# Rotating the queries of an attention and feed-forward kernel in blocks of four heads, moved through DRAM

## Chip, cores, metric

One core of a Trainium2 chip. The metric is the device time of one execution in microseconds (us); the lower the better.

## What is computed

Per batch (B = 4) of 256 tokens with 256 features: a cross-attention with 16 heads whose keys and values come from a latent of 64, with a rotated part of 64 beside the plain part of each head, then a feed-forward layer with ternary weights and quantised activations. Cut to what the change touches:

```python
kv_c = kv @ W_kvc                      # latent of 64
q_c = q @ W_dq                         # latent of 96
q_nope = (q_c @ W_uq).reshape(b, lq, H, HD).transpose(0, 2, 1, 3)   # H 16, HD 128
q_rope = (q_c @ W_qr).reshape(b, lq, H, R).transpose(0, 2, 1, 3)    # R 64
k_rope = kv_c @ W_kr
q_rope = _rope(q_rope, lq)             # [x1*cos - x2*sin, x1*sin + x2*cos], x1, x2 the halves of 32
k_rope = _rope(k_rope, lk)
scores = (einsum('bhqd,bkhd->bhqk', q_nope, k_nope) + einsum('bhqr,bkr->bhqk', q_rope, k_rope)) * scale
scores = where(good, scores, NEG)      # a window of 8 segment numbers
out = einsum('bhqk,bkhd->bqhd', softmax(scores), v).reshape(b, lq, H * HD) @ W_o
x = x + tanh(g_xattn) * out
x = x + tanh(g_ffn) * ffn(layernorm(x))  # 256 -> 1024 -> 256, silu, gelu, layer norm, quantised twice
```

## The kernel before

Tokens are worked on in F = 8 tiles of 128, and each tile in STEPS = 4 steps of GROUP = 4 heads, so there are N = 32 steps. Step n belongs to tile f = n // 4 and has k = n % 4. All segment numbers in use lie in the first 128 keys, so the branch with 128 keys runs (kts = 1). Head pairs share one operand: for an even head the partitions 0 to 63 of qcat and kcat hold the plain part (folded into the latent's 64) and 64 to 127 the rotated one; for an odd head it is the other way round.

Each engine has its own program, in an order written out by hand, and they meet at semaphores. One step n of the loop:

- TensorE: scores(n) (L878 adds the mask, L883 the four products with qcat), transpose_probs(n-2) (L895), project of a later step (L805 into bank_pair, four matmuls with wcat; L808 into bank_swap, two with wswap, whose columns are those of wcat with the halves exchanged), values(n-2) (L907). Between them lie the parts of the feed-forward of earlier tiles: transpose_x (L930) and up (L939) in step 0, attn_out (L920) in steps 1 and 2, transpose_h (L949) in steps 2 and 3, down (L959) in step 3.
- VectorE: softmax_max(n) (L1289), invert_sums(n-1) (L1297), turn_step: L1137 multiplies bank_pair by the cosines (ones for the plain parts) into qcat, L1141 multiplies bank_swap by the signed sines into turned. Then layer_norm_h (L1230, L1231) in step 0, the quantising of the hidden row (L1182, L1190, L1192, L1193) with silu (L1212) in step 1, the residual and its quantising in step 2, moments and output (L1260, L1264) in step 3. first_product (L1206) comes ahead of step 1.
- ScalarE: copy_latT (L633), copy_probT (L642), exponentials (L654, four with their sums). In step 1 the squares of the hidden row (L621) come before and the tanh (L606) behind the exponentials, in step 2 copy_h (L626) and gelu (L611) behind them; gelu needs another table, and so do the next exponentials. In tile 0 the absolute values of both feed-forward weights (L587) follow the exponentials of steps 0 and 1.
- GpSimd: normalise(n-1) (L485), add_rope_step: L406 and L408 add turned to the two rotated halves of qcat, one after the other. Roots (L430, L437) and factors (L456) for the quantisations.
- SyncE: all loads but four, in one queue, then the store of each output tile (L377).

The projection runs AHEAD = 2 steps ahead of the scores that use it: project in step n is that of step n + 2, and turn_step and add_rope_step likewise. scores(n) waits for pair_done, the end of L408. The next project waits for pair_turned, the end of L1141.

Before the loop: inputs are normed and transposed, keys and values projected and the keys rotated (turn_keys, L1075 to L1079; their latents copied by ScalarE in two copies of 64x256, L536 and L537), and the head weights are transposed, copied by ScalarE (L573, L574) and folded (L794), with project(0, 0) between fold(1) and fold(2) and project(0, 1) behind them. ScalarE's copies to L573 follow directly on the squares of the distances (L550).

## Time and profile before

| | |
|---|---|
| Three runs, median | 251.71 us (251.49 to 251.83) |
| The profiled execution: its time | 251.6 us |
| Its span | 249.8 us, 4518 instructions |
| TensorE busy | 210.2 us, 84% |
| TensorE weight loads (beside it) | 167.5 us, 67% |
| VectorE busy | 187.7 us, 75% |
| ScalarE busy | 155.6 us, 62% |
| GpSimd busy | 149.7 us, 60% |
| DMA | 12.40 MB, nearly all in the first 42 us |
| Granted TensorE clock, mean | 0.937; full up to the last fifth |

The span is what the engines' records cover; the execution's own time has 1.8 us more around it. The busy time of an engine is the sum of its instructions' durations, and neighbours on one engine can overlap at their ends, so where one instruction's cost is wanted, the distance between two starts says more. A released wait stands behind a row in brackets: the idle time of the engine just before that instruction, and the instruction that ended it. A matmul of fp32 has two records. The chain that ended last runs through TensorE for 45% of the span, VectorE 19%, GpSimd 12%, ScalarE 9%.

### The profile page before, as it was taken

To read this page: it belongs to the slowest core of one execution; us is meant where nothing else is said; L and a number is where in the kernel's file an instruction comes from. 1 tells how busy PE (TensorE), PEld (TensorE's weight loads), DVE (VectorE), ACT (ScalarE), POOL (GpSimd) and SP (SyncE) were. 2 spreads that over 40 slices of the span, in tenths; PEclk is the share of its full clock that TensorE was granted. 3 is DMA by queue.
4 is the path that set the end of the run, shared out by engine and by line. 5 is a ranking of instruction groups with operands and counts; after the bars stand their busy time and mean duration, and the time that the engine had idled before them with its cause. 6 is when DMAs were issued, how large, how long until landed. Compare 5 with 4: busy or idle time off the path is not lost.

```text
span 249.8 us, 4518 instructions
## 1 busy us (share of the span) xinstructions
PE 210.2 (84%) x1452; PEld 167.5 (67%) x1452; DVE 187.7 (75%) x430; ACT 155.6 (62%) x455; POOL 149.7 (60%) x222
## 2 busy tenths in 40 slices
PE   1799899999999999998998999899899746834453
PEld 1677788688978877886786888678678632513231
DVE  2587556689786679988988998898899842779761
ACT  2256627737557597759559875965887593849021
POOL 0415726639776469788787878778787832062630
PEclk9999999999999999999999999999999996775557
DMA  6999994000000000000000000000000000000001
GB/s 194 286 213 184 318 385 189 0 0 3 1 3 0 3 3 0 3 0 0 24 1 0 25 0 0 4 21 0 4 22 0 3 0 21 0 0 0 24 22 31
DMA packets 11357, 12.40 MB, mean 50 GB/s; under 512 B 3936, under 2 KB 10336, under 8 KB 11104
## 3 DMA queue, kind: packets, MB, share of 16 engines
q1 hardware_dynamic: 10432, 11.44, 16.6%
q10 hardware_dynamic: 896, 0.61, 0.8%
q8 instruction: 14, 0.23, 0.4%
q14 instruction: 15, 0.12, 0.2%
HBM read 11.00 MB, written 1.05 MB: 48 GB/s over the span
## 4 chain that ended last, share of the span: by engine, by line
PE 45%; DVE 19%; POOL 12%; issue 11%; ACT 9%; DMA 1%; DVEq 0%; SPq 0%; POOLq 0%
PE bank_pair L805 7%; PE bank_score L883 5%; PE bank_ff L920 4%; POOL h_small L430 4%; PE bank_lat L907 4%; PE bank_swap L808 3%; DVE z L1206 3%; PE bank_prob L895 3%; DVE h L1230 3%; POOL prob_room L485 3%; DVE neg_max L1289 3%; ACT prob_room L654 3%; PE bank_ff L959 3%; PE bank_ff L939 2%; POOL qcat L408 2%
## 5 line engine op out<-in xcount | busy, mean ns | idle before, releaser
L654 ACT ACTIVATE prob_room<-bank_score,neg_max 128x128 f32<-128x128 f32 x128 | 45.3, 369 | 23.5 <-DVE neg_max L1289 23.5
L485 POOL TENSOR_TENSOR prob_room<-prob_room,rsum 128x512 f32<-128x512 f32 x32 | 33.3, 1041 | 26.0 <-DVE rsum L1297 25.8
L406 POOL TENSOR_TENSOR qcat<-qcat,turned 64x256 f32<-64x256 f32 x32 | 30.8, 963 | 11.9 <-DVE turned L1141 11.8
L883 PEld LDWEIGHTS bank_score<-kcat,qcat 128*128 128x128 f32 x256 | 33.7, 192 | 2.3
L805 PE MATMUL bank_pair<-qcT,wcat 96*128 96x128 f32 x256 | 34.0, 276 | 0.0
L883 PE MATMUL bank_score<-kcat,qcat 128*128 128x128 f32 x256 | 33.7, 275 | 0.0
L642 ACT COPY probT_room<-bank_prob 128x512 f32<-128x512 f32 x32 | 19.0, 594 | 22.4 <-PE bank_prob L895 22.4
L920 PE MATMUL bank_ff<-m_sb,latT 128*128 128x256 f32 x128 | 31.9, 395 | 0.0
L805 PEld LDWEIGHTS bank_pair<-qcT,wcat 96*128 96x128 f32 x256 | 31.1, 192 | 0.4 <-DVE wcat L1126 0.2
L408 POOL TENSOR_TENSOR qcat<-qcat,turned 64x256 f32<-64x256 f32 x32 | 29.6, 924 | 2.5
L1137 DVE TENSOR_TENSOR qcat<-bank_pair,cst 128x512 f32<-128x512 f32 x32 | 21.6, 674 | 10.5 <-PE bank_swap L808 10.5
L907 PE MATMUL bank_lat<-probT_room,kvc 128*64 128x256 f32 x128 | 21.3, 413 | 9.2 <-ACT probT_room L642 9.2
L920 PEld LDWEIGHTS bank_ff<-m_sb,latT 128*128 128x128 f32 x128 | 23.9, 196 | 6.2 <-issue 3.4
L654 ACT ACTIVATION_READ_ACCUMULATOR prob_room<-bank_score,neg_max 128x1 f32 x128 | 26.4, 206 | 0.0
L1289 DVE TENSOR_REDUCE neg_max<-bank_score 128x4 f32<-128x512 f32 x32 | 21.8, 682 | 3.5 <-PE bank_score L883 3.3
L895 PE MATMUL bank_prob<-cst,prob_room 128*128 128x128 f32 x128 | 19.8, 278 | 1.8 <-POOL prob_room L485 1.8
L949 PE MATMUL bank_ff<-cst,h 128*128 128x128 f32 x64 | 12.2, 335 | 9.9 <-DVE h L1193 9.8
L808 PE MATMUL bank_swap<-qcT,wswap 96*128 96x128 f32 x128 | 19.5, 275 | 0.0
L949 PEld LDWEIGHTS bank_ff<-cst,h 128*128 128x128 f32 x64 | 9.2, 172 | 13.6 <-DVE h L1193 13.6
L895 PEld LDWEIGHTS bank_prob<-cst,prob_room 128*128 128x128 f32 x128 | 15.2, 144 | 2.5 <-POOL prob_room L485 2.4
L808 PEld LDWEIGHTS bank_swap<-qcT,wswap 96*128 96x128 f32 x128 | 16.9, 192 | 0.0
L907 PEld LDWEIGHTS bank_lat<-probT_room,kvc 128*64 128x64 f32 x128 | 6.4, 137 | 15.5 <-ACT probT_room L642 10.6
(163 smaller groups left out, 436.6 us busy)
## 6 DMA issues: line engine op xcount, KB each, us to landing
wo<-in_L_xattn_W_o SPq DMA_DIRECT2D x1, 2048.0 KB, 19.5
w_sb<-in_L_ffn_w SPq DMA_DIRECT2D x2, 1024.0 KB, 9.9
out_x<-y SPq DMA_DIRECT2D x8, 128.0 KB, 1.7
wuq<-in_L_xattn_W_uq SPq DMA_DIRECT2D x1, 768.0 KB, 11.5
ctx_all<-in_ctx ACTq DMA_DIRECT2D x2, 256.0 KB, 5.0
x_all<-in_x SPq DMA_DIRECT2D x2, 256.0 KB, 4.7
cst<-in_consts SPq DMA_DIRECT2D x1, 512.0 KB, 7.0
x_all<-in_x SPq DMA_DIRECT2D x1, 512.0 KB, 8.2
```

The costliest lines, as they stand in the source:

```text
L406: nc.gpsimd.tensor_tensor(odd, odd, add_odd, ALU.add).then_inc(pair_half, 1)
L408: nc.gpsimd.tensor_tensor(even, even, add_even, ALU.add).then_inc(pair_done, 1)
L485: nc.gpsimd.tensor_tensor(p, p, rsum[:, k % 2, :].unsqueeze(2).broadcast_to([P, GROUP, kts * P]), ALU.mult).then_inc(prob_scaled, 1)
L654: last = nc.scalar.activation(prob_of(n, kts)[:, j, :], src[:, j, :], ACT.Exp, bias=neg_max[:, k % 2, j:j + 1], accum_out=esum[:, k % 2, j ...
L805: nc.tensor.matmul(bank_pair[:, (2 * j + e) * P:(2 * j + e + 1) * P], wcat[:, 2 * k + j, e, :], src, start=True, stop=True)
L808: last = nc.tensor.matmul(bank_swap[:, j * P:(j + 1) * P], wswap[:, 2 * k + j, :], src, start=True, stop=True)
L883: last = nc.tensor.matmul(bank[:, j * kts * P:(j + 1) * kts * P], qcat[:, k, hh // 2, hh % 2, :], kcat[:, b, hh % 2, 0:kts * P], start=Fal ...
L895: last = nc.tensor.transpose(bank_prob[:, j * P:(j + 1) * P], prob_of(n, kts)[:, j, kt * P:(kt + 1) * P], eye)
L907: last = nc.tensor.matmul(bank_lat[o * KVC:(o + 1) * KVC, 0:2 * P].rearrange("p (j s) -> p j s", j=2), kvc1[:, b * KT + kt, :], probT[:, k ...
L920: last = nc.tensor.matmul(bank_ff[:, 0, 0:D], latT[:, j, :], m_sb[:, j, :], start=(j == 0), stop=(j == PAIRS - 1))
L1137: nc.vector.tensor_tensor(qcat[:, k, :, :, :], bank_pair[:, :].rearrange("p (j e s) -> p j e s", j=2, e=2), cos, ALU.mult)
L1289: nc.vector.tensor_reduce(neg_max[:, k % 2, :], score_banks(k, kts), AX.X, ALU.max, negate=True).then_inc(max_done, 1)
```

## The change

The queries' rotated parts are projected apart from the plain ones. For a step, two matmuls with wrope give the first halves of the rotated parts of four heads in one block of 128 partitions and the second halves in another, both in bank_swap; two matmuls with wnope give the plain parts in bank_pair. VectorE multiplies the two blocks by a table of cosines and sines in one operation (product), GpSimd adds once (rotated). The rotated parts now lie on other partitions than qcat wants, so SyncE stores the block to a DRAM tensor (rope_stage), waits for it, and loads it back in two transfers of 64 partitions to qcat (move_rope). The plain parts are copied from bank_pair to qcat by ScalarE, in two copies of 64 partitions (copy_nope), behind the exponentials of a step. AHEAD is 3 instead of 2. The rotated parts of the keys are kept in the order that the new transfers give. The tables grow from 1152 to 1920 columns. W_qr is loaded once, in whole rows, instead of twice in pieces of 64 columns. The two gates are loaded earlier, and the loads of w1, w2, b1, ln_g, ln_b and b2 are issued from ScalarE's queue, between its squares of the distances and its fold copies. The stores of the output wait in SyncE's program behind a later move.

Cut to its core: declarations, the keys' side and the preparation of wrope (which reorders W_qr's columns by halves of a head) are left out. product holds [partition, slot, first or second half of the result, first or second half of the input, token], rotated the two sums.

```diff
--- before.py
+++ after.py
     freq = (np.float32(1.0) / np.float32(10000.0) ** (np.arange(half, dtype=np.float32) / np.float32(half)))
     ang = np.arange(S, dtype=np.float32)[None, :] * freq.astype(np.float32)[:, None]
     cos, sin = np.cos(ang).astype(np.float32), np.sin(ang).astype(np.float32)
-    one = np.ones((KVC, S), np.float32)
+    cos4, sin4 = np.concatenate([cos] * 4), np.concatenate([sin] * 4)
     c = np.zeros((P, CONSTS), np.float32)
     c[:, EYE:EYE + P] = np.eye(P, dtype=np.float32)
     c[:, IOTA:IOTA + S] = np.arange(S, dtype=np.float32)[None, :] + LOOKBACK / 2
-    c[:, COS:COS + S] = np.concatenate([one, cos, cos])
-    c[:, COS + S:COS + 2 * S] = np.concatenate([cos, cos, one])
-    c[:, SIN:SIN + S] = np.concatenate([-sin, sin, -sin, sin])
+    for i, part in enumerate((cos4, -sin4, sin4, cos4)):
+        c[:, ROT + i * S:ROT + (i + 1) * S] = part
+    c[:, COS:COS + S] = np.concatenate([np.stack([cos, cos], 1).reshape(R, S)] * 2)
+    c[:, SIN:SIN + S] = np.concatenate([np.stack([-sin, sin], 1).reshape(R, S)] * 2)
     return c
 
 
...
             load(cst[:, IOTA:CONSTS], consts[:, IOTA:CONSTS], "rope")
             with nc.allow_non_contiguous_dma(reason="1024 token numbers"):
                 load(seg_i[:, :], itok.rearrange("b (t p) -> p (b t)", p=P), "seg")
+            load(gates[:, 0:1], g_xattn.partition_broadcast(P), "gate0")
+            load(gates[:, 1:2], g_ffn.partition_broadcast(P), "gate1")
             load_group(load, x_all, x_v, 2, "x")
             load_group(load, ctx_all, ctx_kv.rearrange("b (t p) d -> p (b t) d", p=P), 2, "ctx")
-            wqr_pair = W_qr.rearrange("k (j e n) -> k j e n", e=2, n=R)
-            load(wcat[:, :, 0, KVC:P], wqr_pair[:, :, 0, :], "wqr0")
-            load(wcat[:, :, 1, 0:R], wqr_pair[:, :, 1, :], "wqr1")
+            load(wqr[:, :], W_qr, "wqr")
             load(wuq[:, :, :], W_uq.rearrange("k (h n) -> k h n", h=H), "wuq")
             load(wuk, W_uk.rearrange("k (h n) -> k h n", h=H), "wuk")
             load(wuk_wuv[KVC:P, :, :], W_uv.rearrange("k (h n) -> k h n", h=H), "wuv")
             load(wo[:, :, :], W_o.rearrange("(h p) n -> p h n", p=P), "wo")
-            load(gates[:, 0:1], g_xattn.partition_broadcast(P), "gate0")
-            load(gates[:, 1:2], g_ffn.partition_broadcast(P), "gate1")
-            load(w1_sb[:, :, :], w1.rearrange("(c p) n -> p c n", p=P), "w1")
-            load(w2_sb[:, :, :], w2.rearrange("(c p) n -> p c n", p=P), "w2")
-            load(b1_bc[:, :], b1.partition_broadcast(P), "b1")
-            load(g_bc[:, :], ln_g.partition_broadcast(P), "g")
-            load(lb_bc[:, :], ln_b.partition_broadcast(P), "lb")
-            load(b2_bc[:, :], b2.partition_broadcast(P), "b2")
 
             out_v = out.rearrange("b (t p) d -> (b t) p d", p=P)
-            for f in range(F):
-                sp.wait_ge(y_done, f + 1)
-                sp.dma_start(out_v[f, :, :], y[:, :]).then_inc(out_stored, 16)
+            staged = stage.rearrange("k (j e i) o s -> k e (i o) j s", j=2, e=2)
+
+            def move_rope(n):
+
+                k = n % STEPS
+                sp.wait_ge(rope_rotated, n + 1)
+                if n >= STEPS:
+                    sp.wait_ge(score_ready, n - STEPS + 1)
+                sp.dma_start(stage[k, :, :, :], rotated[:, k, :, :]).then_inc(rope_staged, 16)
+                sp.wait_ge(rope_staged, 16 * (n + 1))
+                for e in range(2):
+                    lo = KVC if e == 0 else 0
+                    sp.dma_start(qcat[lo:lo + R, k, :, e, :], staged[k, e, :, :, :]).then_inc(rope_moved[k], 16)
+
+            def store(c):
+                sp.wait_ge(y_done, c + 1)
+                sp.dma_start(out_v[c, :, :], y[:, :]).then_inc(out_stored, 16)
+
+            for n in range(N):
+                move_rope(n)
+                c = (n - 4 * STEPS - AHEAD) // STEPS
+                if c >= 0 and n == c * STEPS + 4 * STEPS + AHEAD:
+                    store(c)
+            for c in range((N - 1 - 4 * STEPS - AHEAD) // STEPS + 1, F):
+                store(c)
             sp.wait_ge(out_stored, 16 * F)
 
         @block.gpsimd
         def _(pool):
-            rope = R // 2
             pool.wait_ge(consts_made, 1)
 
             def input_root(b):
...
                 add_rope(kcat[KVC:P, b, 0, :], kcat[0:R, b, 1, :], turned[KVC:P, b % 2, :], turned[0:R, b % 2, :], b)
 
             def add_rope_step(f, k):
-                t = turned[:, k % 2, :].rearrange("p (j s) -> p j s", j=2)
-                add_rope(qcat[KVC:P, k, :, 0, :], qcat[0:R, k, :, 1, :], t[KVC:P, :, :], t[0:R, :, :], B + step_no(f, k))
+                n = step_no(f, k)
+                pool.wait_ge(rope_multiplied, n + 1)
+                if f > 0:
+                    pool.wait_ge(rope_moved[k], MOVED * f)
+                nc.gpsimd.tensor_tensor(rotated[:, k, :, :], product[:, k % 2, :, 0, :], product[:, k % 2, :, 1, :],
+                                        ALU.add).then_inc(rope_rotated, 1)
 
             for k in range(AHEAD):
                 add_rope_step(0, k)
...
             copy_keys(B - 1)
             square_dists(B - 1)
 
+            load(w1_sb[:, :, :], w1.rearrange("(c p) n -> p c n", p=P), "w1")
+            load(w2_sb[:, :, :], w2.rearrange("(c p) n -> p c n", p=P), "w2")
+            load(b1_bc[:, :], b1.partition_broadcast(P), "b1")
+            load(g_bc[:, :], ln_g.partition_broadcast(P), "g")
+            load(lb_bc[:, :], ln_b.partition_broadcast(P), "lb")
+            load(b2_bc[:, :], b2.partition_broadcast(P), "b2")
 
             for i in range(H // 4):
                 act.wait_ge(wt_ready, i + 1)
...
                 nc.scalar.copy(wuqT[:, i % 2, :, :], input_banks(i)[:, 0, 0:4 * QC].rearrange("p (h c) -> p h c", h=4))
                 nc.scalar.copy(wukvT[:, 4 * i:4 * i + 4, :],
                                input_banks(i)[:, 1, :].rearrange("p (h c) -> p h c", h=4)).then_inc(wt_copied, 1)
+
+            def copy_nope(f, k):
+                n = step_no(f, k)
+                act.wait_ge(nope_ready, n + 1)
+                if f > 0:
+                    act.wait_ge(score_ready, n - STEPS + 1)
+                src = bank_pair[:, 0:2 * P].rearrange("p (j s) -> p j s", j=2)
+                nc.scalar.copy(qcat[0:KVC, k, :, 0, :], src[0:KVC, :, :])
+                nc.scalar.copy(qcat[KVC:P, k, :, 1, :], src[KVC:P, :, :]).then_inc(nope_copied, 1)
+
+            for k in range(AHEAD):
+                copy_nope(0, k)
 
             act.wait_ge(in_sems["gate0"], 16)
             act.wait_ge(in_sems["gate1"], 16)
...
                             copy_h(f - 3, 1)
                         if k == 1 and there(f, 3):
                             sum_squares(f - 3)
-                        if f < F:
-                            exponentials(f, k, kts)
+                        exponentials(f, k, kts)
+                        if step_no(f, k) + AHEAD < N:
+                            copy_nope(*ahead(f, k))
                         prepare(f, k)
                         if k == 1 and there(f, 2):
                             tanh(f - 2)
...
 
             def project(f, k):
 
-                s = B + step_no(f, k)
-                pe.wait_ge(pair_turned, s)
+                n = step_no(f, k)
                 src = qcT[:, f * P:(f + 1) * P]
+                if n:
+                    pe.wait_ge(rope_multiplied, n)
+                else:
+                    pe.wait_ge(pair_turned, B)
+                for e in range(2):
+                    last = nc.tensor.matmul(bank_swap[:, e * P:(e + 1) * P], wrope[:, k, e, :], src, start=True, stop=True)
+                last.then_inc(rope_ready, 1)
+                if n:
+                    pe.wait_ge(nope_copied, n)
                 for j in range(2):
-                    for e in range(2):
-                        nc.tensor.matmul(bank_pair[:, (2 * j + e) * P:(2 * j + e + 1) * P], wcat[:, 2 * k + j, e, :], src,
-                                         start=True, stop=True)
-                for j in range(2):
-                    last = nc.tensor.matmul(bank_swap[:, j * P:(j + 1) * P], wswap[:, 2 * k + j, :], src, start=True, stop=True)
-                last.then_inc(pair_ready, 1)
+                    last = nc.tensor.matmul(bank_pair[:, j * P:(j + 1) * P], wnope[:, 2 * k + j, :], src, start=True, stop=True)
+                last.then_inc(nope_ready, 1)
 
             transpose_weights(0)
             transpose_weights(1)
...
             nc.tensor.matmul(bank_ff[0:1, 0, 0:P], farthest[:, 0:1], eye, start=True, stop=True).then_inc(far_turned, 1)
             pe.wait_ge(fold_copied, 2)
             project(0, 1)
+            pe.wait_ge(fold_copied, 3)
+            project(0, 2)
 
             pe.wait_ge(wide_ready, 1)
             pe.wait_ge(fold_copied, H // 4)
...
                 lag = 1 if kts == 1 else 0
                 if n > lag:
                     pe.wait_ge(exp_done, n - lag)
-                pe.wait_ge(pair_done, B + n + 1)
+                if n == 0:
+                    pe.wait_ge(pair_done, B)
+                pe.wait_ge(nope_copied, n + 1)
+                pe.wait_ge(rope_moved[k], MOVED * (f + 1))
                 per = GROUP // kts
                 b = f // TILES
                 for i in range(kts):
...
 
             def copy_fold(i):
                 dve.wait_ge(fold_ready, i + 1)
-                src = fold_bank(i)[0:QC, 0:4 * KVC].rearrange("k (j e c) -> k j e c", e=2, c=KVC)
-                nc.vector.tensor_copy(wcat[:, 2 * i:2 * i + 2, 0, 0:KVC], src[:, :, 0, :])
-                nc.vector.tensor_copy(wcat[:, 2 * i:2 * i + 2, 1, R:P], src[:, :, 1, :]).then_inc(fold_copied, 1)
+                nc.vector.tensor_copy(wnope[:, 2 * i:2 * i + 2, :],
+                                      fold_bank(i)[0:QC, 0:4 * KVC].rearrange("k (j c) -> k j c", j=2)).then_inc(fold_copied, 1)
 
             def turn_step(f, k):
 
-                s = B + step_no(f, k)
+                n = step_no(f, k)
                 at = (f % TILES) * P
-                cos = cos_tab[:, :, at:at + P].unsqueeze(1).broadcast_to([P, 2, 2, P])
-                sin = sin_tab[:, at:at + P].unsqueeze(1).broadcast_to([P, 2, P])
-                dve.wait_ge(pair_ready, s + 1)
-                if f > 0:
-                    dve.wait_ge(score_ready, step_no(f, k) - STEPS + 1)
-                nc.vector.tensor_tensor(qcat[:, k, :, :, :], bank_pair[:, :].rearrange("p (j e s) -> p j e s", j=2, e=2),
-                                        cos, ALU.mult)
-
-                dve.wait_ge(pair_done, max(B, s - 1))
-                nc.vector.tensor_tensor(turned[:, k % 2, :].rearrange("p (j s) -> p j s", j=2),
-                                        bank_swap[:, 0:S].rearrange("p (j s) -> p j s", j=2), sin, ALU.mult).then_inc(pair_turned, 1)
+                dve.wait_ge(rope_ready, n + 1)
+                if n >= 2:
+                    dve.wait_ge(rope_rotated, n - 1)
+                x = bank_swap[:, 0:2 * P].rearrange("p (e s) -> p e s", e=2).unsqueeze(1).broadcast_to([P, 2, 2, P])
+                nc.vector.tensor_tensor(product[:, k % 2, :, :, :], x, rot_tab[:, :, :, at:at + P],
+                                        ALU.mult).then_inc(rope_multiplied, 1)
 
             copy_fold(0)
             copy_fold(1)
...
             link(nc.vector.tensor_reduce(farthest[0:1, 1:2], bank_ff[0:1, 0, 0:P], AX.X, ALU.max))
             nc.vector.tensor_scalar(wide[:, :], farthest[0:1, 1:2], mid * mid, None, ALU.is_gt).then_inc(wide_ready, 1)
             turn_step(0, 1)
+            turn_step(0, 2)
 
             def prepare(f, k):
 
```

## Rows read from the trace of the kernel before

**Rows 1.** Busy time by tile: span, then PE, PEld, DVE, ACT, POOL, clock, DMA.

```profile
37.13:54.29 17.16, 16.27 (x134) 13.39 (x135) 11.69 (x23) 10.52 (x36) 8.61 (x11) 1.00 0.20 76
54.29:74.13 19.84, 19.84 (x167) 16.89 (x166) 16.72 (x32) 11.41 (x40) 15.87 (x19) 1.00 0.01 2
74.13:93.04 18.91, 18.91 (x142) 15.60 (x140) 12.38 (x29) 14.46 (x48) 11.88 (x18) 1.00 0.01 2
93.04:116.08 23.04, 21.18 (x156) 17.24 (x155) 20.88 (x48) 16.50 (x52) 18.45 (x28) 1.00 0.00 1
138.15:160.22 22.07, 20.90 (x157) 17.21 (x155) 19.83 (x45) 16.35 (x52) 17.44 (x27) 1.00 0.02 8
182.28:204.35 22.07, 18.27 (x132) 14.52 (x130) 17.42 (x39) 16.34 (x52) 16.22 (x24) 1.00 0.02 7
```

**Rows 2.** Timeline of TensorE in the tile from 138.15 (start, duration, idle before).

```profile
139.69 1.06 PE L805 MATMUL bank_pair<-qcT,wcat 96*128 96x128 f32 x8
140.59 0.61 PE L808 MATMUL bank_swap<-qcT,wswap 96*128 96x128 f32 x4
...
158.75 0.65 PE L907 MATMUL bank_lat<-probT_room,kvc 128*64 128x256 f32 x4 [1.17 <-ACT probT_room L642]
```

**Rows 3.** The same tile, timeline of VectorE.

```profile
147.04 0.65 DVE L1137 TENSOR_TENSOR qcat<-bank_pair,cst 128x512 f32<-128x512 f32 x1
147.62 0.41 DVE L1141 TENSOR_TENSOR turned<-bank_swap,cst 128x256 f32<-128x256 f32 x1
...
151.66 0.21 DVE L1190 TENSOR_SCALAR h_small<-h_small 128x1 f32<-128x1 f32 x1 [0.72 <-POOL h_small L437]
```

**Rows 4.** The same tile, timeline of ScalarE.

```profile
147.07 0.37 ACT L654 ACTIVATE prob_room<-bank_score,neg_max 128x128 f32<-128x128 f32 x1 [0.77 <-DVE neg_max L1289]
...
148.45 1.16 ACT L606 ACTIVATE tanh_z<-z 128x512 f32<-128x512 f32 x2
...
157.85 0.35 ACT L633 COPY latT<-bank_lat 128x256 f32<-128x256 f32 x1
158.11 0.59 ACT L642 COPY probT_room<-bank_prob 128x512 f32<-128x512 f32 x1
```

**Rows 5.** Timeline of ScalarE during the weight preparation.

```profile
23.76 0.91 ACT L550 ACTIVATE z<-cst,neg_seg 128x256 f32<-128x256 f32 x2
24.66 0.37 ACT L536 COPY kcat<-bank_lat 64x256 f32<-64x256 f32 x1
25.04 0.37 ACT L537 COPY kcat<-bank_lat 64x256 f32<-64x256 f32 x1
...
28.16 0.48 ACT L573 COPY wuqT<-bank_score 128x384 f32<-128x384 f32 x1 [0.35 <-PE bank_score L786]
```

**Rows 6.** Timeline of GpSimd at the start of the loop.

```profile
35.65 0.72 POOL L408 TENSOR_TENSOR qcat<-qcat,turned 64x256 f32<-64x256 f32 x1
...
42.48 1.04 POOL L485 TENSOR_TENSOR prob_room<-prob_room,rsum 128x512 f32<-128x512 f32 x1
```

**Rows 7.** Timeline of SyncE's queue: two issues of loads.

```profile
13.28 0.59 SPq L346 DMA_DIRECT2D wo<-in_L_xattn_W_o  x1
...
27.09 3.49 SPq L346 DMA_DIRECT2D w_sb<-in_L_ffn_w  x2
```

**Rows 8.** DMA issues: KB each, median us to landing.

```profile
wo<-in_L_xattn_W_o SPq DMA_DIRECT2D x1, 2048.0 KB, 19.5
...
out_x<-y SPq DMA_DIRECT2D x8, 128.0 KB, 1.7
```

**Rows 9.** Three stretches: the loads' rate, and TensorE's clock about an idle stretch.

```profile
36.00:39.00 3.00, 2.70 (x24) 2.51 (x23) 1.58 (x3) 0.00 (x0) 1.26 (x3) 1.00 1.02 407
218.00:220.00 2.00, 0.00 (x0) 0.00 (x0) 1.53 (x7) 0.29 (x1) 0.90 (x3) 1.00 0.00 0
222.00:224.00 2.00, 1.58 (x4) 0.43 (x4) 1.81 (x4) 1.98 (x4) 0.99 (x4) 0.50 0.00 0
```

**Rows 10.** Timeline of TensorE: the second step's mask matmul.

```profile
39.60 0.39 PE L878 MATMUL bank_score<-mask,eye_b 128*128 128x512 bf16 x1
```

53 lines of the change are left out of this document (35 added, 18 removed).

## Prediction

> **What bounds the kernel now.** I read four views in order. First the busy time by tile: the loop over eight tiles runs from 37.13 to 204.35 us of a span of 249.8. In tiles 1 and 2 TensorE is busy for the whole of 19.84 and 18.91 us, so a microsecond of TensorE is worth a microsecond there. From tile 4 on a tile takes 22.07 us though TensorE is busy 20.90, VectorE 19.83, GpSimd 17.44 and ScalarE 16.35 of it: no engine is full, a chain through all four sets the period [rows 1]. Second, that chain in the timelines of one such tile. VectorE waits 0.72 us for GpSimd's root before it can quantise the hidden row [rows 3]. ScalarE waits 0.77 us for VectorE's maximum [rows 4]. At the end of the tile TensorE waits 1.17 us for ScalarE, which by then has come through exponentials, a copy of the quantised row, a table load, gelu and the copy of the probabilities [rows 2, 4]. Third, ScalarE in the weight preparation, because the change puts six DMA issues there [rows 5]. Fourth, the DMA queue and the rate of the loads at the start of the loop [rows 7 to 9].
>
> **TensorE and VectorE, removed.** Six projection matmuls of a step take 0.90 us for the four of bank_pair (139.69 to 140.59) and 0.44 for the two of bank_swap (140.59 to 141.03, the next start), 0.22 each [rows 2]. Afterwards there are two rope and two nope matmuls, of the same 96x128 form: 0.44 us less a step, 1.77 a tile. VectorE loses the 0.41 us product of bank_swap; the 0.65 us product of 128x512 stays as one of the same size [rows 3]. GpSimd has one addition of 128x256 for two of 64x256 at 0.72: bounded by 0.72 and the 1.04 of a 128x512 operation [rows 6], I take 0.8, some 0.64 us less a step. The weight copies on VectorE become fewer; they lie beside other work and count nothing.
>
> **ScalarE, added.** Every step gets a pair of copies of 64x256 from PSUM, behind the exponentials. The nearest rows are the copies to kcat, of that very form: the first starts at 24.66, just where the two squares before it end (23.76 + 0.91), the second at 25.04, 0.38 later, and lasts 0.37 [rows 5]. So two such copies don't overlap, while ordinary neighbours do: the copy to latT lasts 0.35, but the next copy starts 0.26 after it (157.85, 158.11) [rows 4]. The pair costs 0.38 + 0.25 = 0.63 us if only the middle is unoverlapped, some 0.1 + 0.38 + 0.37 = 0.86 if both of its ends are. I take 0.78, nearer to the upper end, since the first copy in the rows shows no overlap with what ran before it. ScalarE gets 3.1 us a tile, to 19.5 of 22.07.
>
> **What the pair does in a steady tile.** Three of its four places count. At step 0 TensorE's nope matmuls now wait for the pair behind the previous exponentials. They end about when the projection ended before, so the feed-forward's transposes, its up product and the second scores start no earlier; above 0.7 us a pair, they start later by the excess. At step 1 VectorE comes to its maximum sooner (fewer projections ahead of it, a shorter turn), and the exponentials start up to 0.83 us earlier: the 0.77 of idle time and the small gap before the squares of the hidden row [rows 4]. But the tanh (148.45) [rows 4] now follows the pair, so the silu on VectorE starts 0.83 less one pair earlier. GpSimd's root, 0.64 us shorter on the way and started earlier, is no longer last, so its 0.72 us [rows 3] goes; what is late next is the tanh. At step 2 a second pair stands between the exponentials and the copy to hqT, with the table load, gelu, latT and probT (157.85, 158.11) [rows 4] behind it, and TensorE's wait of 1.17 us at their end. Sum: 0.83 + 0.72 - 2 pairs = 1.55 - 1.56 = 0, less 0.08 at step 0. So tiles 4 to 6, where 4 x 0.44 of TensorE seemed to be won, come out at +0.1 each; with pairs of 0.63 they win 0.3 each, with 0.86 they lose 0.35 each.
>
> **The other tiles.** Tile 7 projects in its first step alone, so the pairs of steps 1 and 2 are missing: 1.55 less, I take -1.5. Tile 1 has a full TensorE and ScalarE at 11.41 of 19.84 [rows 1]: -1.77. Tile 2 has ScalarE at 14.46 of 18.91, and the pairs bring it to 17.6, so not all is passed on: between 0.5 and 1.77, I take -1.3. Tile 3 takes 23.04 and falls into the steady chain: between 0 and 1.77, I take -0.6. In tile 0 ScalarE also takes the absolute values of both weights, and two pairs come ahead of the probabilities that TensorE waits for; the 1.33 us of three projections go into that: 0, within 1 either way.
>
> **The start.** Before, the first scores start at 37.13 and the second step at 39.60 [rows 1, 10]. Three things come in their way. (a) ScalarE issues six loads in front of its first fold copy, which starts at 28.16 [rows 5]. An unblocked issue of such a load takes SyncE's queue up to 0.59 us; the two of w1 and w2 take 3.49, most of it waiting behind wo [rows 7]. At 0.5 each, an estimate below the 0.59 of wo's, that is 3.0 us on ScalarE, which has 0.35 idle there: the first fold copy starts at 30.8, and the projections come 2.3 us later, since small gaps between the copies take up the rest. The old block was complete at 36.37 (35.65 + 0.72) [rows 6]; the new path to it lacks 0.89 of projection, 0.41 on VectorE and 0.64 on GpSimd, so it stands ready at 36.37 - 1.94 + 2.3 = 36.7. (b) It must travel. A store of the same 128 KB takes 1.7 us to landing [rows 8]; SyncE waits for it, then issues two loads. Idle, that is 1.7, two issues at some 0.35 and 1.7 again: the scores could start at 40.8. (c) The engines aren't idle: they move 407 GB/s at a busy share of 1.02 from 36 to 39 [rows 9]. The store stands in SyncE's queue behind wo, whose landing comes 19.5 us after its issue at 13.28, at 32.8 [rows 7, 8]. ScalarE's queue now competes with wo from 28 on. In the 4.8 us from 28 to 32.8 at most 1.95 MB of wo were moved at that rate; I take 1.65, the rate being lower early. At equal bytes for both queues wo would land at 28 + 3.3 / 0.407 = 36.1; behind nearly all of the other queue's 3.6 MB, at some 40. I take 37.5, then 1.7 for the store and 1 to 2 us more for both trips among the loads: first scores at 43. The second block's store is issued only after the first's loads, so the second step starts at 45.0 where it was 39.60: +5.4, bounded by +3.5 (nothing in the way but the trips: the second block's 4.1 us begin at 39.1, when the first's loads are issued) and +7.
>
> The Trainium skill, "DMA: Bandwidth & Descriptors", in the section on queues, rings and completion order, says that each DMA engine serves the queues that have work in turn, a packet at a time. No row before shows two loaded queues; by that rule alone wo would land between my two figures, and the start would stay at about +5.4.
>
> (d) While the first blocks travel TensorE is idle for some 3 to 4 us. Its granted clock is 1.00 in a stretch with no matmul at 218 and 0.50, the lower of its two levels (1.2 GHz), from 222 on, behind it [rows 9]. If that happens at 43, the first steps' matmuls take double: +0.7, between 0 and 1.5. The Trainium skill, "TensorE: Matmul & The Clock Gate", in the section on the clock gate, says that idleness brings the lower clock and that work must earn the higher back; it would charge this start and nothing else in the loop, as the row does.
>
> In the steady part the trips cost nothing. A block made in step n is wanted three steps later, over 13 us by the shortest tile of 17.16 for four steps [rows 1], against trips of 4 to 5. If that cover were gone, every step would carry the difference. The tail behind 204.35 has no projection, and I leave it. The stores of y now wait for a move first, a step at most, with four steps to spare.
>
> **The sum.** Start +5.4, tile 0 0, tile 1 -1.77, tile 2 -1.3, tile 3 -0.6, tiles 4 to 6 +0.2, tile 7 -1.5, clock +0.7: +1.1 us on the profiled execution's own 251.6. That stands 0.1 below the median of the runs, 251.71; so I forecast 252.8.
>
> **The rivals.** *The start is cheap.* If wo has landed before the first store and the trips take what they take when idle, the start costs +3.5 and the clock stays up: 252.8 - 1.9 - 0.7 = 250.2, and with pairs of 0.63, at 0.35 less in each of tiles 4 to 6, 249.1. For it: the store of 1.7 us, and the single wqr load with long rows in place of two of short ones, which brings wo forward. Against it: the rate of 407 GB/s. *The late loads block.* wo lands at 40 and the clock falls for longer: +1.6 + 0.8, 255.2. This is the slower side at its worst, and it decides from where the first block's landing passes 43. *ScalarE becomes the bound.* Pairs of 0.86, and what waits behind them in tiles 1 to 3 as well: +0.25 x 4 + 1, 254.8. *The change doesn't do what it says:* the trips are not covered by three steps, as they take over 13 us; each step then waits for its block, and the time passes 265. Nothing in the rows points there.
>
> **How the numbers follow.** The forecast has 0.42 (251.3 to 254.3), the cheap start 0.34, the blocking loads 0.13, ScalarE as bound 0.09, uncovered trips 0.02. Within 0.2% of 251.7, which is about what a measurement can tell from no change, lie 0.01 of the second and 0.10 of the first; another 0.02 of the first lie below. Faster 0.35, same 0.11, slower 0.54. The range from 249.0 to 256.3 leaves out some 0.1 on each side.
>
> **What would show it.** The gap between 37 and the second scores, +5.4. The fold copies' first start, at 30.8 instead of 28.16. Pairs on ScalarE that hold 0.78 us from the last exponential's end to the next operation. Tiles 1 to 7 at 18.1, 17.6, 22.4, 22.1 and, the last, 20.6 us. No waits for a block after tile 0. The prediction is wrong above all if the first scores start before 41, or if a steady tile is shorter than 21.5, which would mean that the chain doesn't run through the copies.

## The result and the profile after

The changed kernel takes 258.43 us in the median of its first four runs (255.55 to 260.58), against 251.77 for the kernel before beside it (251.49 to 252.09): ratio 1.023, 95% interval 1.014 to 1.031. It is slower, by about 2% in the runs that the ratio uses (one of the four, 260.58, was in a slower state and is not among them), and the time lies outside the range of the prediction. Its four runs spread over 5 us, those of the kernel before over 0.6. The profiled execution is its fastest, 255.55 us: 3.9 above the 251.6 of the profiled one before, and 2.9 below its own median. So two questions stand: where the 3.9 come from, and what the other executions do on top.

Busy time by tile, from one first scores to the next (columns as in [rows 1]):

```profile
43.27:61.92 18.65, 17.14 (x119) 14.21 (x120) 9.81 (x18) 12.30 (x40) 4.55 (x6) 0.84 0.21 64
61.92:81.69 19.77, 18.35 (x151) 15.15 (x149) 15.81 (x28) 14.38 (x50) 11.77 (x15) 1.00 0.18 54
81.69:101.09 19.40, 17.34 (x124) 13.89 (x123) 11.13 (x29) 16.98 (x56) 9.48 (x15) 1.00 0.18 56
101.09:122.94 21.85, 19.09 (x139) 15.59 (x139) 18.49 (x44) 19.54 (x60) 14.69 (x25) 1.00 0.16 51
122.94:144.42 21.48, 19.09 (x139) 15.57 (x138) 17.95 (x40) 19.17 (x60) 13.04 (x22) 1.00 0.18 56
144.42:166.45 22.03, 19.64 (x139) 15.81 (x138) 17.95 (x40) 19.71 (x62) 13.34 (x22) 0.97 0.19 61
166.45:188.76 22.31, 19.89 (x138) 16.51 (x138) 17.93 (x40) 18.83 (x59) 13.10 (x21) 0.95 0.16 48
```

TensorE is busy 18.35 of 19.77 us in tile 1 where it was full, and 19.09 of 21.48 in tile 4 where it had 20.90 of 22.07 [rows 1]: the 1.77 us of matmuls are gone, and most of them came back as idle time. Tile by tile, beside the forecast:

| | before | after | change | forecast |
|---|---|---|---|---|
| first scores | 37.13 | 43.27 | +6.1 | +5.4 with the second step |
| tile 0 | 17.16 | 18.65 | +1.5 | 0, clock +0.7 |
| tile 1 | 19.84 | 19.77 | -0.1 | -1.77 |
| tile 2 | 18.91 | 19.40 | +0.5 | -1.3 |
| tile 3 | 23.04 | 21.85 | -1.2 | -0.6 |
| tiles 4 to 6 | 66.20 | 65.82 | -0.4 | +0.2 |
| tile 7 to the span's end | 67.52 | 64.94 | -2.6 | -1.5 |
| sum | 249.8 | 253.7 | +3.9 | +1.1 |

The start in the same execution, timelines of ScalarE and of SyncE's queue (compare [rows 5, 7]), then of TensorE:

```profile
26.66 0.60 ACTq L557 DMA_DIRECT2D w_sb<-in_L_ffn_w  x1
27.29 0.49 ACTq L557 DMA_DIRECT2D b_bc<-in_L_ffn_b  x1
...
29.27 0.48 ACT L616 COPY wuqT<-bank_score 128x384 f32<-128x384 f32 x1 [1.96 <-PE bank_ff L842]
```

```profile
35.49 0.36 SPq L391 DMA_DIRECT2D rope_stage<-rotated  x1
40.24 1.29 SPq L395 DMA_DIRECT2D qcat<-rope_stage  x2
41.58 0.59 SPq L391 DMA_DIRECT2D rope_stage<-rotated  x1
43.67 1.23 SPq L395 DMA_DIRECT2D qcat<-rope_stage  x2
```

```profile
43.27 0.59 PE L943 MATMUL bank_score<-mask,eye_b 128*128 128x512 bf16 x1 [4.67 <-DMA qcat<-rope_stage]
...
47.06 0.63 PE L943 MATMUL bank_score<-mask,eye_b 128*128 128x512 bf16 x1
```

The six issues hold ScalarE from 26.25 to 29.22. The first block's store is issued at 35.49; SyncE gets past it 4.75 us later, then issues two loads (1.29 us), and 3.03 us after the first of them the scores start. The second block repeats this: its store can only be issued behind the first block's loads, its own loads at 43.67. By the same 3.03 us it could be used at 46.70. The second step starts at 47.06, with no idle time of TensorE before it: TensorE is still busy with the first step, at half clock. What the store didn't wait for is wo: its load was issued at 11.30 and landed 18.7 us later, at 30.0, 5.5 us ahead of the store. In its way were the late loads from ScalarE's queue, the last of which landed at about 40.5 (issued at 28.77, 11.7 us to landing).

```profile
11.30 0.59 SPq L362 DMA_DIRECT2D wo<-in_L_xattn_W_o  x1
...
wo<-in_L_xattn_W_o SPq DMA_DIRECT2D x1, 2048.0 KB, 18.7
```

The stretches show the clock (same columns as above):

```profile
39.00:42.00 3.00, 0.00 (x0) 0.00 (x0) 0.00 (x0) 0.58 (x3) 0.69 (x1) 1.00 0.11 35
42.00:45.00 3.00, 1.73 (x8) 1.67 (x9) 0.00 (x0) 0.00 (x0) 0.00 (x0) 0.57 0.21 68
45.00:48.00 3.00, 3.00 (x15) 2.85 (x15) 1.38 (x2) 1.67 (x9) 0.73 (x1) 0.50 0.28 87
...
163.00:166.00 3.00, 1.58 (x10) 0.95 (x11) 2.26 (x9) 2.98 (x6) 2.27 (x4) 0.88 0.17 50
166.00:169.00 3.00, 3.00 (x17) 2.75 (x15) 1.14 (x3) 2.66 (x12) 0.20 (x1) 0.55 0.21 67
```

It falls to 0.50, the lower level (1.2 GHz), behind the idle stretch at the start, as forecast, and again in the middle of the loop, at about 165, which was not. That second fall straddles two tiles: tile 5 and tile 6 have a mean clock of 0.97 and 0.95 and are 0.55 and 0.83 us longer than tile 4, 1.38 us together. It follows the 1.91 us wait that ends tile 5; the same wait ends tile 4, and the clock stays at 1.00 behind it.

In a steady tile a pair of copies holds ScalarE for 0.77 us (132.47 to 133.24), and the tanh stands behind it; then the gelu's part and TensorE's wait at the tile's end, 1.91 us where it was 1.17 [rows 2, 4]:

```profile
132.47 0.37 ACT L626 COPY qcat<-bank_pair 64x256 f32<-64x256 f32 x1
132.85 0.37 ACT L627 COPY qcat<-bank_pair 64x256 f32<-64x256 f32 x1
133.24 1.15 ACT L661 ACTIVATE tanh_z<-z 128x512 f32<-128x512 f32 x2
...
142.31 0.59 ACT L697 COPY probT_room<-bank_prob 128x512 f32<-128x512 f32 x1
```

```profile
142.95 0.65 PE L972 MATMUL bank_lat<-probT_room,kvc 128*64 128x256 f32 x4 [1.91 <-ACT probT_room L697]
```

### The profile page after: what moved, and what is told of

The parts are those of the page before. It is cut to its first block, busy times and chain, and to the rows that moved or that the text cites. A ratio compares the mean times of both kernels' runs of the same rounds, so it can differ in the third digit from the quotient of the medians.

```text
span 253.7 us, 4402 instructions
## 1 busy us (share of the span) xinstructions
PE 197.9 (78%) x1317; PEld 156.4 (62%) x1324; DVE 173.5 (68%) x392; ACT 178.0 (70%) x519; POOL 117.8 (46%) x191
## 2 busy tenths in 40 slices
DMA packets 23726, 21.19 MB, mean 84 GB/s; under 512 B 3920, under 2 KB 22608, under 8 KB 23472
## 4 chain that ended last, share of the span: by engine, by line
PE 31%; ACT 28%; DVE 17%; issue 13%; DMA 4%; POOL 3%; ACTq 1%; SPq 0%; DVEq 0%; POOLq 0%
ACT prob_room L709 10%; PE bank_ff L985 4%; PE bank_score L948 4%; PE bank_ff L1004 3%; PE bank_lat L972 3%; DVE z L1271 2%; DVE neg_max L1348 2%; ACT L709 2%; ACT probT_room L697 2%; DMA rope_stage<-rotated 2%; PE bank_prob L960 2%; ACT hqT L681 2%; ACT qcat L627 2%; PE bank_ff L1024 2%; ACT z L666 2%
## 5 line engine op out<-in xcount | busy, mean ns | idle before, releaser
L948 PEld LDWEIGHTS bank_score<-kcat,qcat 128*128 128x128 f32 x256 | 36.4, 205 | 2.6
L452 POOL TENSOR_TENSOR rotated<-product 128x256 f32<-128x256 f32 x32 | 31.1, 973 | 14.5 <-DVE product L1199 14.5
L948 PE MATMUL bank_score<-kcat,qcat 128*128 128x128 f32 x256 | 36.3, 288 | 0.0
L1199 DVE TENSOR_TENSOR product<-bank_swap,cst 128x512 f32<-128x512 f32 x32 | 21.5, 671 | 2.9 <-PE bank_swap L863 2.0
L868 PE MATMUL bank_pair<-qcT,wnope 96*128 96x128 f32 x128 | 20.5, 284 | 1.7 <-ACT qcat L627 1.7
L863 PE MATMUL bank_swap<-qcT,wrope 96*128 96x128 f32 x128 | 20.2, 281 | 0.4 <-DVE product L1199 0.4
L868 PEld LDWEIGHTS bank_pair<-qcT,wnope 96*128 96x128 f32 x128 | 17.3, 196 | 2.5 <-ACT qcat L627 2.4
L863 PEld LDWEIGHTS bank_swap<-qcT,wrope 96*128 96x128 f32 x128 | 17.4, 197 | 0.8 <-issue 0.8
L681 ACT ACTIVATE hqT<-bank_ff 128x512 bf16<-128x512 f32 x16 | 9.5, 600 | 10.6 <-PE bank_ff L1014 10.5
L1265 DVE SCALAR_TENSOR_TENSOR z<-bank_ff,x_deq,b_bc 128x512 f32<-128x512 f32 x16 | 11.2, 740 | 8.2 <-PE bank_ff L1004 8.2
## 6 DMA issues: line engine op xcount, KB each, us to landing
wo<-in_L_xattn_W_o SPq DMA_DIRECT2D x1, 2048.0 KB, 18.7
```

Of the source, the lines that this page charges most:

```text
L452: nc.gpsimd.tensor_tensor(rotated[:, k, :, :], product[:, k % 2, :, 0, :], product[:, k % 2, :, 1, :], ALU.add).then_inc(rope_rotated, 1)
L863: last = nc.tensor.matmul(bank_swap[:, e * P:(e + 1) * P], wrope[:, k, e, :], src, start=True, stop=True)
L868: last = nc.tensor.matmul(bank_pair[:, j * P:(j + 1) * P], wnope[:, 2 * k + j, :], src, start=True, stop=True)
L948: last = nc.tensor.matmul(bank[:, j * kts * P:(j + 1) * kts * P], qcat[:, k, hh // 2, hh % 2, :], kcat[:, b, hh % 2, 0:kts * P], start=Fal ...
L1199: nc.vector.tensor_tensor(product[:, k % 2, :, :, :], x, rot_tab[:, :, :, at:at + P], ALU.mult).then_inc(rope_multiplied, 1)
```

## The experiments

All against the kernel before on the same chip (its medians lay between 251.29 and 251.68). "First scores" and tile lengths come from each one's profiled execution.

**Where the spread is: repeat.** No edit.

> The changed kernel again, nothing edited. Its four executions so far lie between 255.6 and 260.6 us where the kernel before lies within 0.6 us. Theory A: the spread is TensorE's clock falling to its lower level at different places of the loop, so a second profile shows the same start (first scores near 43.3 us) and another number or place of stretches at 0.50 inside the tiles; the time is 255 to 261. Rival B: the spread comes from the loads at the start (when the first moved block lands), so the first scores start at another time, by as much as the whole difference, and the tiles repeat within 0.2 us.

258.41 us (257.13 to 259.69). In its profiled execution, 259.69, tiles 0 to 4 are those of the table to 0.02 us (18.65, 19.78, 19.40, 21.86, 21.47), and the first scores start at 47.47 instead of 43.27. So the 4.1 us between the two executions are all in the start. Part of them comes before ScalarE issues any late load: its first issue is at 27.38 instead of 26.25, and the loads issued long before land later (wo 24.2 us after its issue for 18.7, the last of the weights to be folded 17.0 for 13.2). From 24 to 27 the DMA engines were as busy but moved less, 351 GB/s in the first execution and 159 in this one:

```profile
24.00:27.00 3.00, 2.55 (x15) 1.77 (x14) 1.03 (x4) 2.03 (x7) 1.44 (x2) 1.00 1.10 351
```

```profile
24.00:27.00 3.00, 3.00 (x15) 2.18 (x14) 1.17 (x3) 2.17 (x6) 1.44 (x2) 1.00 1.04 159
```

Then one issue on ScalarE took 1.69 us where it had 0.49:

```profile
28.57 1.69 ACTq L557 DMA_DIRECT2D b_bc<-in_L_ffn_b  x1
...
32.06 0.48 ACT L616 COPY wuqT<-bank_score 128x384 f32<-128x384 f32 x1 [3.62 <-PE bank_ff L842]
...
36.15 0.48 ACT L616 COPY wuqT<-bank_score 128x384 f32<-128x384 f32 x1 [2.25 <-PE bank_score L842]
```

Behind that 3.62 us of idle time the preparation itself ran slower: the third fold copy comes 4.09 us after the first, where it came 2.74 after it in the changed kernel's first profile (29.27, 32.01). The granted clock goes with it. It was 1.00 from 30 to 36 in the first profile, behind one wait of 1.87 us for ScalarE; here it is 0.50, behind 1.55 us for the late weights and 1.92 us for ScalarE:

```profile
30.00:33.00 3.00, 1.16 (x7) 0.81 (x5) 0.31 (x1) 0.94 (x3) 1.62 (x2) 0.50 1.13 353
```

So the later start of 4.20 us is 1.13 us before the first issue, 1.66 in the issues and 1.35 in the fold at half clock, and 0.06 behind it.

**The late loads' part alone, in the kernel before: before_act.**

```diff
 # before.py: SyncE's queue
-            load(w1_sb ...) ... load(b2_bc ...)      (six loads behind the gates)
 # ScalarE, behind square_dists(B - 1)
+            load(w1_sb ...) ... load(b2_bc ...)
```

> The kernel before with one part of the change alone: the six late loads are issued from ScalarE's queue, ahead of its first fold copy, and nothing else. Theory (the issues on ScalarE are half of the later start, and a source of the spread): the first fold copy starts at 29.3 to 32 where it was 28.16, so the first scores come at 38.5 to 41 instead of 37.13, all tiles as before (22.07 in the steady part), 253.5 to 255, ratio 1.007 to 1.013, with a spread of over 1 us where the kernel before has 0.5. Rival (the late start is all in the trips through DRAM, the issues are absorbed by slack in the preparation): 251.5 to 252, ratio 1.000.

254.77 us (252.64 to 257.73), ratio 1.011 (1.002 to 1.021). In its profile the fold copy starts at 29.76 and the scores at 38.77, +1.6; the tiles are those of before. This part alone costs 1.2 to 4.9 us in three of its four runs, 6.3 in the fourth. In the same round 18 of 19 runs of the kernel before lie within 1.5 us, and one at 253.47. The rival, that slack takes the issues up, is out.

**More in ScalarE's queue: wo_act.** wo is issued from ScalarE too, ahead of w1.

> The load of wo issued from ScalarE's queue ahead of w1 instead of from SyncE's queue, nothing else. Theory A (the first store stands behind wo in SyncE's queue: it took 4.75 us, 35.49 to 40.24, where the median is 1.7): the store lands 1.7 to 2.7 us after its issue and the first scores start at 40.7 to 41.8 instead of 43.3; the time falls by 1.5 to 2.5 us. Rival B (the engines are full, whichever queue holds the loads): the store still takes over 4 us and the first scores stay at 43 or later; the seventh issue on ScalarE puts the fold copies 0.5 us later.

264.27 us, ratio 1.051 (1.046 to 1.056). An issue now blocks ScalarE for as long as bulk loads are queued:

```profile
26.95 2.12 ACTq L556 DMA_DIRECT2D w_sb<-in_L_ffn_w  x1
...
29.10 3.94 ACTq L556 DMA_DIRECT2D w_sb<-in_L_ffn_w  x1
...
35.27 0.48 ACT L616 COPY wuqT<-bank_score 128x384 f32<-128x384 f32 x1 [7.67 <-issue]
```

First scores at 49.41. By the time of the first store, 44.53, the loads were done, and it landed in 1.77 us: the store that took 4.75 us was slow for the loads beside it. Here too the fold ran at a granted clock of 0.50, from 33 to 42.

**No trips: notrip.** The moves are left out (the rotated parts are missing from the scores, which wait for GpSimd's sum instead; qcat is set to zero at the start).

```diff
-                sp.dma_start(stage[k, :, :, :], rotated[:, k, :, :]).then_inc(rope_staged, 16)
-                ...
-                    sp.dma_start(qcat[lo:lo + R, k, :, e, :], staged[k, e, :, :, :]) ...
-                pe.wait_ge(rope_moved[k], MOVED * (f + 1))
+                pe.wait_ge(rope_rotated, n + 1)
```

> The moves through DRAM left out: GpSimd's sum stays where it is, the scores wait for that sum and read rotated parts of zero from qcat (so the rotated parts are missing from the scores), everything else is the same. This is the price of the trips. Theory A (trips cost at the start alone): the first scores start at 38.8 to 39.5, no clock falls there, tiles 1 to 7 last what they last in the changed kernel (19.8, 19.4, 21.9, then 21.5), and the time is 250.5 to 252.5. Rival B (the trips also hold up tiles 1 and 2, or the DMA's writes slow the engines): tiles 1 and 2 shrink towards 18.1 and 17.6, and the time is below 249.5.

254.75 us, ratio 1.015 (1.007 to 1.022). First scores 40.20, second step 42.19, tile 0 17.75; tiles 1 to 3 19.77, 19.38, 21.84, as with the trips. So the trips cost some 3.7 us, all of it before tile 1. No later tile is shorter without them (tiles 4 to 6 are 22.17, 22.16 and 22.13, with two falls of the clock). 3.4 us of loss remain without any trip.

**Where the late loads go.** Three orders of the changed kernel's own: all six on SyncE's queue behind wo (loads_sp); all six on ScalarE behind its first three pairs (loads_after); w1 and w2 on SyncE behind wo, the four broadcasts behind the fourth block's move (loads_two).

```diff
 # loads_two
             load(wo[:, :, :], ...)
+            load(w1_sb ...); load(w2_sb ...)
...
                 move_rope(n)
+                if n == 3:
+                    load(b1_bc ...); load(g_bc ...); load(lb_bc ...); load(b2_bc ...)
```

> The six late loads (w1, w2, b1, ln_g, ln_b, b2) issued from SyncE's queue behind wo, as in the kernel before; all else as in the changed kernel. Theory A (the issues on ScalarE hold up the fold copies and through them the projections, by 1.1 us in one execution and 3.9 in another, and this is the spread): the fold copies start at 27.5 to 28.5 us, the spread between runs falls under 1.5 us; but SyncE can't take the first store before all loads are issued and moved, so the first scores start at 44 to 46 and the time is 255 to 259. Rival B (the spread comes from the trips): it stays at 2.5 us or more.

258.87 us, ratio 1.031 (1.024 to 1.038). The fold copy is back at 27.91, yet the first store needs 6.3 us behind the loads, and the scores start at 43.48: what ScalarE gave back the queue took.

> The six late loads still issued from ScalarE's queue, but behind its first three pairs of copies instead of ahead of its fold copies. Theory A (start cost = blocked issues + the first trip among the loads): the fold copies start at 27.5 to 28.5, wo lands alone before the first store is issued at 34 to 35, the store lands in about 2 us, the first scores start at 38.5 to 40.5, TensorE idles under 1.5 us and keeps its clock, and the time is 249.5 to 252.5 with a spread under 1.5. Rival B (w1 comes too late for its absolute values, or the store still waits): first scores after 42, or a wait for w1 in tile 0 that takes the gain back; time above 254.

260.70 us, ratio 1.035 (1.031 to 1.039). The first scores come at 38.71, the earliest with trips. But then the second and third block travel among the late loads:

```profile
33.87 0.36 SPq L391 DMA_DIRECT2D rope_stage<-rotated  x1
35.63 1.29 SPq L395 DMA_DIRECT2D qcat<-rope_stage  x2
36.97 0.59 SPq L391 DMA_DIRECT2D rope_stage<-rotated  x1
41.82 1.23 SPq L395 DMA_DIRECT2D qcat<-rope_stage  x2
43.09 0.59 SPq L391 DMA_DIRECT2D rope_stage<-rotated  x1
50.75 1.77 SPq L395 DMA_DIRECT2D qcat<-rope_stage  x2
```

A store landed in 1.76 us alone, and in 4.85 and 7.66 among 3.6 MB of loads. The second step starts at 50.06. From 30 to 36 the DMA engines now moved only 17 and 44 GB/s: there is room for w1 and w2.

> The changed kernel with all late loads on SyncE's queue: w1 and w2 directly behind wo, in the stretch in which the DMA engines were found idle (30 to 36 us when they weren't there), and the four rows broadcast to all partitions (1.6 MB) only behind the fourth block's move. ScalarE issues none of them. Theory (the late start is the bulk loads in the way of the first three blocks, plus the issues on ScalarE): fold copy at 27.6 to 28, first store issued at 34 and landed by 37, first scores at 38.7 to 40.5, second step at 40.5 to 43, the clock falls little or not at all, tile 0 some 18; whole 250.5 to 253, ratio 0.995 to 1.005, with a spread under 1 us. Rival (any bulk load queued behind wo keeps the first store waiting for its last packet): first scores at 42 to 43.5, 256 to 258, ratio 1.02 to 1.03.

254.25 us (251.58 to 257.22, too scattered for an interval). First scores 38.86, second step 42.28, as expected; but the fifth block's store, issued behind the four broadcasts, took 6.6 us, and tile 0 came out at 21.19. Tile 1 gave most of it back, with 17.99: together they are 0.76 us longer than in the changed kernel. The broadcasts one behind each of the fifth to eighth moves, loads_spread:

> The changed kernel with the same load order as best_spread alone (no split, tanh as in the change). Theory (the start costs what of it the loads' order makes, and it is separate from ScalarE's pairs): first scores 39 to 41, second step by 44, tile 0 some 18.6, the later tiles as in the changed kernel (19.77, 19.4, 21.9, 21.5 to 22.3): 251 to 253, ratio 0.998 to 1.006. Rival: as loads_two, tile 0 at 21.2, 254, ratio 1.012.

254.11 us (250.69 to 258.25). The profiled execution, 250.69, has first scores at 39.89 and tile 0 at 17.61. The better order is seen there up to the end of tile 0; tile 1, among the broadcasts, is 20.49. The four runs fall into two groups, 250.69 and 252.02, 256.2 and 258.25, and so do those of loads_two (251.58 and 251.98, 256.52 and 257.22). Only the lowest of each was profiled. No late load is issued from ScalarE here, so what makes the slower pairs must be something else; no trace shows it.

**The clock at the start: warm, warm_long.** 18 and 40 transposes of the identity on TensorE while it waits for the first block.

```diff
+            for i in range(40):
+                nc.tensor.transpose(bank_lat[:, (i % 4) * P:(i % 4 + 1) * P], eye, eye)
```

> 18 transposes of the identity into a free bank on TensorE (about 4 us) between the projection of step 2 and the first scores, that is, in the idle time before the first moved block; the output is the same. Theory A (the idle stretch drops the clock, and the half clock from 43 to 49 us costs the second step): the first scores stay at 43.3, the second step starts at 45.3 to 46 instead of 47.1, the third at 49.5 to 50.5 instead of 52.1, and the time falls by 1.5 to 2.5 us. Rival B (the second step waits for its own moved block, whose loads are issued at 43.7): the second step stays at 46.5 to 47.1 with idle time before it, and the time falls by less than 0.7.

> The changed kernel with 40 more transposes of the identity on TensorE (0.11 us each, 4.4 us) in the stretch in which it waits for the first block; nothing reads their result. Theory (the start's half clock, granted at 42 to 48 behind the idle stretch, costs about 1.5 us: the first step takes 3.79 us where it took 2.47 before): the clock stays at 1.00 to 48 and the second step comes 2.3 to 2.6 us after the first scores, tile 0 at 17.2 to 17.5: 1.2 to 1.5 us faster than the changed kernel in like executions. Rival (the first step is paced by the second block's trip, not by the clock): the clock stays up, the second step still comes 3.3 to 3.8 us after the first, no gain.

18 took 2 us, too little to fill the wait; the clock still fell (259.53 us), and in the loop it fell three times where it had fallen once. 40 took 4.53 us, and the clock held:

```profile
42.00:45.00 3.00, 3.00 (x30) 3.00 (x29) 0.00 (x0) 0.64 (x3) 0.73 (x1) 1.00 0.29 89
45.00:48.00 3.00, 3.00 (x28) 2.95 (x27) 0.82 (x2) 0.10 (x1) 0.00 (x0) 1.00 0.28 87
```

The whole took 258.77 us, ratio 1.026 (1.023 to 1.029): no gain. The test isn't clean. The second step came 2.00 us after the first (47.87 after 45.87), sooner than the 2.3 to 2.6 of the theory, but the transposes ended at 45.87, 2.4 us after the first block can have come (its loads were issued at 40.43), so the second had time to arrive as well; tile 0 took 19.32. Other rows bound what the half clock costs at this place. In the changed kernel the second block could be used at 46.70 and TensorE was ready at 47.06: a full clock would have brought the second step forward by 0.36 us at most. And tile 0 lasts 18.64 to 18.65 us in the changed kernel, repeat, loads_sp, warm and pair_late, whether its second step comes 3.39 or 3.79 us after the first.

**ScalarE's pairs: nopair, split, pair_late.** nopair leaves the copies of the plain parts out (they are missing from the scores). split gives one of each pair to VectorE. pair_late moves the pair of each step 1 behind the tanh:

```diff
+                        late = k == 1 and there(f, 2)
-                        if step_no(f, k) + AHEAD < N:
+                        if step_no(f, k) + AHEAD < N and not late:
                             copy_nope(*ahead(f, k))
                         prepare(f, k)
                         if k == 1 and there(f, 2):
                             tanh(f - 2)
+                        if step_no(f, k) + AHEAD < N and late:
+                            copy_nope(*ahead(f, k))
```

> ScalarE's copies of the plain parts left out, and the waits for them (the plain parts of the queries are missing from the scores): the price of the pairs, 28 of them in the loop. Theory A (the pairs set the steady tiles and a part of tile 1 and 2): tile 1 falls from 19.8 to 18.7 to 19.1 us, tile 2 from 19.4 to 18.0 to 18.4, tiles 4 to 6 from 21.5 to 20.0 to 20.4. Rival B (VectorE's ternary steps and the feed-forward chain set them, the pairs only fill gaps): tile 1 stays above 19.4 and tiles 4 to 6 above 21.0.

> One of the two copies of a pair moved to VectorE, behind its product; the other stays on ScalarE. ScalarE is relieved of some 0.38 us a step, VectorE gets 0.43 or less, with 17.95 of 21.48 us of it busy. Theory A (ScalarE's chain is the bound, at two places of a steady tile): tiles 4 to 6 fall to 20.9 to 21.2 us. Rival B (VectorE's own chain through layer norm, z and quantising is as tight): they stay at 21.4 to 21.9, since what ScalarE wins VectorE loses.

> The changed kernel with ScalarE's pair of copies of each step 1 placed behind the tanh instead of ahead of it. Theory (in a steady tile the pair ahead of the tanh delays the silu, the quantised row and with them the gelu and the copy of the probabilities for which TensorE waits): each of tiles 3 to 6 is 0.4 to 0.8 us shorter, 21.0 to 21.4, and the whole 2 to 3 us faster than the changed kernel, 255 to 256 us, ratio 1.015 to 1.02. Rival (the other pair, at step 2, sets the period alone; the tanh has slack): tiles stay at 21.5, ratio 1.025 or so. The start and its spread stay as they are, first scores at 43 to 47.

| tile | 1 | 2 | 3 | 4 | whole, us | ratio |
|---|---|---|---|---|---|---|
| before | 19.84 | 18.91 | 23.04 | 22.07 | 251.7 | |
| changed | 19.77 | 19.40 | 21.85 | 21.48 | 258.4 | 1.023 to 1.026 |
| pair_late | 19.77 | 19.39 | 21.08 | 20.70 | 253.38 | 1.008 (1.005 to 1.012) |
| split (clock 0.53 from 142 to the end of tile 4) | 19.52 | 18.94 | 21.48 | 21.89 | 253.92 | 1.010 (1.006 to 1.013) |
| nopair | 19.01 | 17.88 | 20.85 | 19.92 | 246.09 | 0.979 (0.976 to 0.981) |

The pairs cost 0.76 us in tile 1, 1.52 in tile 2 and 1.56, two pairs, in tile 4. In tile 0, which is not in the table, they cost 1.36: 18.65 with them, 17.29 without. Without any pair the changed kernel is faster than the one before, with them slower: over the whole they cost some 12 us. Placing one of them behind the tanh gives 0.78, one pair, back in tile 4, and nothing in tile 2 (tile 1 has no tanh yet, so nothing is moved there). VectorE's wait for the tanh shows it, by the waits of one tile (us, times, longest), first of the changed kernel, then of pair_late:

```profile
DVE z L1271 <- ACT tanh_z L661: 1.3, 1, 1.3
```

```profile
DVE z L1274 <- ACT tanh_z L661: 0.5, 1, 0.5
```

pair_late gained more than the 2 to 3 us expected of it, 5.0 by the medians. Its tiles 3 to 6 are 4.49 us shorter in all, of which four pairs are 3.1. Most of the rest is the clock: in its trace it doesn't fall from 100 to 193 us, and tiles 4 to 6 take 20.70 each.

**All together: best, best_spread, best_apart.** Split, the late pair, and w1 and w2 behind wo; the broadcasts all behind the fourth move, behind the fifth to eighth, or behind the fifth, seventh, ninth and eleventh.

> The load order of loads_two, one copy of each pair on VectorE (as in split), and ScalarE's remaining copy of each step 1 behind the tanh (as in pair_late). If the three causes add up (start 3 to 4 us, pairs split 4.5 us in all, tanh 1.5 to 2 us): first scores at 39 to 40.5, tiles 18.2, 19.5, 18.9, 21.3, then 21.0 to 21.3 each, 245 to 248 us, ratio 0.975 to 0.985, faster than both kernels. Rival (the split copies make VectorE's maxima late, so that the tanh's place wins nothing, and the start stays at 43): 252 to 254, ratio 1.005.

> The kernel of best, with the four broadcast rows issued one behind each of the fifth to eighth moves instead of all behind the fourth. In best the fifth block's store took 6.6 us among them and tiles 0 and 1 came out at 21.22 and 20.53. Theory (a block in transit must meet no more than one bulk load): tile 0 at 18.2 to 18.8, tile 1 at 19.5, the rest as in best (18.9, 21.2, 20.8 three times), first scores at 39 to 41, so 3 to 4 us less than best: 247.5 to 249.5, ratio 0.985 to 0.992. Rival (each broadcast delays the block behind it by nearly as much, and the delay passes on): 250 to 252, ratio 0.995 to 1.002. What is left of the spread is then w1 and w2 behind wo: first scores differ by up to 2 us between executions.

> The kernel of best_spread, with the four broadcast rows behind the fifth, seventh, ninth and eleventh moves, one at every other move, instead of behind four in a row. In best_spread every move with a broadcast ahead of it held SyncE's queue for 6.2 to 6.7 us, four in a row, while tile 1 wants one every 4.9, and tile 1 came out at 21.20. Theory (SyncE's queue, not the single block's delay, is what tile 1 waited for; a move without a broadcast takes 3.4 us and lets the queue catch up): tile 1 at 19.5, the rest as in best_spread, 247 to 248, ratio 0.983 to 0.987. Rival (each delayed block passes its delay on by itself): tiles 1 and 2 together as before, 248.9, ratio 0.990.

251.55 us, ratio 0.995 (0.990 to 0.999), where 245 to 248 was expected: tiles 2 to 6 came as expected or shorter, tiles 0 and 1 at 21.22 and 20.53; 248.87, 0.990 (0.988 to 0.992), with 18.21 and 21.20; 247.60, 0.986 (0.982 to 0.990), with 18.18 and 19.53. In best_spread each move with a broadcast ahead held SyncE's queue over 6 us, where a step of tile 1 comes every 4.9 us when nothing delays it (a quarter of best_apart's 19.53):

```profile
54.90 0.38 SPq L394 DMA_DIRECT2D rope_stage<-rotated  x1
59.61 1.24 SPq L398 DMA_DIRECT2D qcat<-rope_stage  x2
60.89 0.59 SPq L363 DMA_DIRECT2D g_bc<-in_L_ffn_ln_g  x1
61.58 0.38 SPq L394 DMA_DIRECT2D rope_stage<-rotated  x1
```

With one at every other move tile 1 is 1.67 us shorter, but tile 2 is 0.97 longer (19.15 for 18.18), and 1.49 us of what best_apart's trace gains lie in the start, so the spacing itself is worth some 0.7 us there; the intervals of the two overlap. The last version beats both kernels, by 1.4% and some 4%.

## Why the prediction was wrong

**The start, nearly right in the profiled execution, too low in the median.** The issues took 3.0 us on ScalarE, as estimated, and the first scores came at 43.27 for 43. That is luck in part, for the parts were off against each other: the issues began at 26.25, so the fold copy started at 29.27 and the block stood ready at 35.47, each over a us before the forecast; its store then took 4.75. Step (c) had the wrong obstacle: it let wo land at 37.5 and hold up the store, but wo had landed at 30.0 (and at 36.6 in repeat, where the store came at 40.00); the store was slow for the late loads of the other queue. In loads_after, with wo landed and no such load yet, the same store takes 1.76 us. Step (c) failed again at the second block: "the second step starts at 45.0" left 2.0 us between the steps, but blocks leave SyncE's queue 3.4 us apart (40.24, 43.67, 46.98), since SyncE waits for a store before it issues the loads. The block could be used at 46.70, and the step started at 47.06, +7.5 for +5.4 and just over its bound of +7. And nothing in the sum let an execution differ from the next. Repeat and wo_act show issues of 1.69 to 3.94 us, and a fold at half clock behind them; I had the 3.49 of [rows 7] and took 0.5 for each, as if ScalarE could not be blocked as SyncE was. The blocking loads (0.13) are nearest to what the median does.

**The clock: seen, wrongly priced.** The +0.7 at the start is 0.36 at most by the rows of the second step. What the clock costs is in the loop: 1.38 us for the one fall in tiles 5 and 6, by the difference from tile 4 in the same trace. I had written that it would fall at the start and nowhere else in the loop. The Trainium skill, "TensorE: Matmul & The Clock Gate", in the section on the clock gate, says that idleness brings the lower clock; the trace agrees in so far as the fall (1.00, then 0.55) follows a wait of 1.91 us, but the same wait at the end of tile 4 brought none. What failed was to look for such idleness only at the start, and not in tiles in which the change takes TensorE's work away. Between 100 and 193 us the clock fell once in the changed kernel and in repeat, twice in notrip, wo_act and warm_long, three times in loads_sp and warm, for 1.2 to 1.4 us each where it can be told from the tiles; in the kernel before, nopair, pair_late, best and best_apart not at all.

**Tile 0, 1.4 us.** "The 1.33 us of three projections go into that: 0, within 1 either way" set the matmuls against ScalarE's added work. It took 18.65 us for 17.16. Without the pairs it takes 17.29: the projections gave nothing back, and the pairs cost 1.36. Without the trips it takes 17.75, so the two causes overlap.

**Tiles 1 and 2: the step that failed in the loop, 3.5 us.** "Full TensorE, ScalarE at 11.41 of 19.84: -1.77" took an engine that is busy throughout for one that nothing can hold up. With the matmuls gone VectorE is next: its two passes over the weights end at 65.34, its maximum goes with their end, and behind it come ScalarE's exponentials, pair, copy to w1T and probabilities, for which TensorE waits 1.09 us.

```profile
61.97 1.71 DVE L1235 TENSOR_SCALAR w_sb<-w_sb 128x2048 f32<-128x2048 f32 x1
63.71 1.63 DVE L1237 TENSOR_SCALAR w1q<-w_sb 128x2048 bf16<-128x2048 f32 x1
65.26 0.68 DVE L1348 TENSOR_REDUCE neg_max<-bank_score 128x4 f32<-128x512 f32 x1
```

And VectorE itself became slower. Its passes over a 128x2048 fp32 tile in place run beside GpSimd's normalisation, and last the longer the more of it they meet. In this tile the first of them took 1.22 us before, where it started behind the normalisation, and takes 1.71 now, where it starts 0.62 us before the normalisation's end (first the changed kernel's row, then two of the kernel before):

```profile
61.55 1.04 POOL L522 TENSOR_TENSOR prob_room<-prob_room,rsum 128x512 f32<-128x512 f32 x1 [5.56 <-DVE rsum L1356]
```

```profile
53.55 1.04 POOL L485 TENSOR_TENSOR prob_room<-prob_room,rsum 128x512 f32<-128x512 f32 x1 [3.57 <-DVE rsum L1297]
...
54.75 1.22 DVE L1176 TENSOR_SCALAR w_sb<-w_sb 128x2048 f32<-128x2048 f32 x1
```

The three such passes of tile 1 took 1.22, 1.44 and 1.64 us before and take 1.71, 1.70 and 1.71 now, 0.82 us more. VectorE's product of bank_swap (0.41 us) no longer stands ahead of them, so they start sooner and meet more of the normalisation; in split, where a copy stands in that place, they take 1.37 and 1.38. Part of what the change saved VectorE is lost in this way.

Even with no pair tile 1 gains 0.83 of the 1.77, and with them 0.07. In tile 2 the gain without pairs is 1.03, and two pairs of 0.76 turn it into +0.5. My bounds (0.5 to 1.77) had no loss in them. The rival "ScalarE becomes the bound" named this, at 0.09, and put 1 us on it.

**Tiles 3 to 6: mechanism right, a term too small.** The pair takes 0.77 us for 0.78, and two of them count in a steady tile: 21.48 - 19.92 = 1.56, as written, one of them because the tanh follows it. GpSimd's root and its 0.72 us [rows 3] are no longer among the tile's waits. But what the change gives without pairs is 22.07 - 19.92 = 2.15, not 1.55. So tile 4 is 0.59 shorter, not 0.1 longer; the clock took most of it back in tiles 5 and 6. (Three tiles at the +0.1 of the text would be +0.3; the sum has +0.2.) Tile 3 won 1.19 for 0.6, and from tile 7 on 2.58 for 1.5.

**The trips after tile 0.** No tile waits for a block: notrip has the same tiles 1 to 3. That holds while nothing else is in the queue; in best_spread, where every move had a broadcast ahead of it, tile 1 was 1.7 us longer than in best_apart.

**What is left open.** The spread. Three parts of it are seen in traces: loads that land later within the first 27 us, issues on ScalarE that last longer behind them, and falls of the clock, in the fold and one to three times in the loop. Why the early loads of repeat moved fewer bytes isn't known. Nor is it why nopair, with the same issues, spreads over 0.8 us in four runs, or what the slower runs of loads_two and loads_spread do, which have no profile. The rounds were run on different chips, and whether the spread depends on the chip wasn't tested.

## What to carry over

A matmul removed from a full TensorE is worth its time only as far as the next engine's chain allows: write down, for each tile, what arrives second, and let the range include a loss. Small transfers on the critical path need a queue and a stretch of their own, so bulk loads go where the traffic is idle. A DMA issue on a computing engine should be priced at what it takes when the queues are full, and placed where nothing waits behind it. Where a change makes TensorE wait longer, its clock can fall there too: in these traces waits of 1.91 us at a tile's end sometimes brought the fall, those of 1.14 and 0.97 us (pair_late, nopair) never.

## What had not been expected of the hardware

- An issue of a late load on ScalarE's queue took 0.37 to 0.60 us in the changed kernel's first profile, and up to 1.69 us in repeat and 2.12 and 3.94 us in wo_act, behind slower or more loads; ScalarE's copies behind it wait.
- A 128 KB store landed in 1.76 us alone and in 4.75 to 7.66 us among 1.6 to 3.6 MB of loads, whichever queue these were issued from (ScalarE's 4.75 and 7.66, SyncE's 6.3 and 6.6).
- A fall of the clock in a steady loop in which TensorE is busy 19.09 of 21.48 us costs 1.2 to 1.4 us, spread over two tiles. In pair_late, busy 19.24 of 20.70 with 1.14 us of wait at the tile's end for 1.91, it didn't fall.
- A pass of VectorE over 128x2048 fp32 in place took 1.09 us plus the time for which GpSimd's normalisation still ran when it started. In twelve passes of four traces (the changed kernel, the one before, split, loads_two) the overlap was 0.62, 0.35, 0.55, 0.29, 0.40 or 0.45 us and the pass 1.71, 1.44, 1.64, 1.38, 1.49 or 1.54; with none it took 1.22, and 1.29 for the pass of tile 0 that has no work of GpSimd beside it. The overlap goes with the difference; that VectorE stands still meanwhile is an inference. GpSimd's addition beside such a pass took 1.71 us for 0.73.
